# Last cross attention of a decoder: the fourth batch's values made between the heads' first maxima

## What is computed

```python
Q = (query @ Wq.T + bq).reshape(b, sq, H, D).transpose(0, 2, 1, 3)
K = (key @ Wk.T + bk).reshape(b, sk, H, D).transpose(0, 2, 1, 3)
V = (value @ Wv.T + bv).reshape(b, sk, H, D).transpose(0, 2, 1, 3)
Q = apply_rope(Q, cos_q, sin_q)
K = apply_rope(K, cos_k, sin_k)
scores = jnp.einsum('bhqd,bhkd->bhqk', Q, K) * SCALE
scores = jnp.where(mask[:, None, None, :] == 0, neg_inf, scores)
attn = jax.nn.softmax(scores, axis=-1)
out = jnp.einsum('bhqk,bhkd->bhqd', attn, V)
```

## Time and profile before

| | us |
|---|---|
| median of 3 runs | 1824.99 |
| lowest and highest | 1813.83 and 1825.43 |
| profiled execution | 1820.29 |
| its span | 1818.4 |
| PE, DVE, ACT, POOL busy, share of the span | 92%, 75%, 57%, 38% |
| projections of this phase | about 1023 to 1128 |
| heads of this phase | about 1127 to 1703 |

### The profile page before, as it was taken

How to read it: one execution, slowest core, us unless ns; L and a number is a source line. 1 busy time by engine, 2 the same in 40 slices (tenths; PEclk the granted TensorE clock), 3 DMA queues, 4 the chain that set the end, 5 groups by cost and what they waited for, 6 DMA issues and landing times. The chain is left out here.

```text
span 1818.4 us, 35284 instructions
## 1 busy us (share of the span) xinstructions
PE 1664.5 (92%) x13824; PEld 912.9 (50%) x13824; DVE 1363.4 (75%) x2337; ACT 1043.8 (57%) x1748; POOL 686.0 (38%) x771
## 2 busy tenths in 40 slices
PE   8998999989999998879999887799999999999996
PEld 4786677668888886423333654122222222223564
DVE  4535888756666665868885779999999999995664
ACT  4322655436566554337777333277888888887542
POOL 2783777024445443423340343215412121111453
PEclk9999999989999998969999999599999999999998
DMA  6163999777877763621110466221201011000001
GB/s 222 55 221 125 318 314 326 241 268 300 310 293 293 290 263 124 205 69 29 37 35 5 152 202 195 49 65 54 73 20 38 20 27 30 19 20 1 24 12 35
DMA packets 111693, 244.55 MB, mean 134 GB/s; under 512 B 27890, under 2 KB 80630, under 8 KB 107908
## 3 DMA queue, kind: packets, MB, share of 16 engines
q1 hardware_dynamic: 84712, 204.56, 32.1%
q0 software_dynamic: 24176, 35.12, 7.3%
q10 hardware_dynamic: 2640, 2.62, 0.4%
HBM read 180.27 MB, written 61.38 MB: 133 GB/s over the span
## 5 line engine op out<-in xcount | busy, mean ns | idle before, releaser
L2205 DVE TENSOR_REDUCE Eh_maxima<-Eh_max 128x2 f32<-128x802 f32 x512 | 474.8, 987 | 21.6 <-PE Eh_max L2077 16.7
L2193 ACT ACTIVATE Eh_probs<-Eh_pair 128x1024 f32<-128x1024 f32 (+1 forms) x288 | 287.5, 998 | 112.5 <-PE Eh_pair L2124 112.4
L2077 PE MATMUL Eh_max<-Eh_KS,Eh_QS 49*128 49x401 f16 x1024 | 197.7, 357 | 44.9 <-DVE Eh_maxima L2205 41.1
L2146 PE MATMUL Eh_av_ps<-Eh_probs,E_V 128*17 128x512 f32 (+1 forms) x1664 | 223.0, 609 | 0.0
L1537 PE MATMUL C_y<-C_x_high,C_W 128*128 128x256 f16 (+1 forms) x1536 | 214.8, 253 | 8.9 <-ACT C_gate L1597 7.4
L1537 PE MATMUL C_y<-C_x_low,C_W 128*128 128x256 f16 (+1 forms) x768 | 180.5, 252 | 0.0
L2193 ACT ACTIVATE Eh_probs<-Eh_single 128x512 f32<-128x512 f32 x272 | 161.7, 594 | 28.0 <-PE Eh_single L2124 27.8
L2205 DVE TENSOR_REDUCE Dh_maxima<-Dh_max 128x2 f32<-128x1024 f32 x128 | 152.0, 1221 | 31.9 <-PE Dh_max L2093 30.7
L1915 POOL DMA_DIRECT2D Eh_KS<-E_kd x64 | 37.1, 579 | 354.0 <-PE Eh_pair L2124 349.1
L2077 PEld LDWEIGHTS Eh_max<-Eh_KS,Eh_QS 49*128 49x128 f16 x1024 | 50.5, 94 | 233.1 <-DVE Eh_maxima L2205 198.2
L1537 PEld LDWEIGHTS C_y<-C_x_high,C_W 128*128 128x128 f16 x1536 | 139.0, 98 | 22.3 <-ACT C_gate L1597 9.6
(11 more groups left out here) (463 smaller groups left out, 3481.2 us busy)
## 6 DMA issues: line engine op xcount, KB each, us to landing
C_W<-w_split SPq DMA_DIRECT2D x24, 3072.0 KB
w_split<-B_w_parts SPq DMA_DIRECT2D x24, 768.0 KB, 8.1
Eh_KS<-E_kd POOLq DMA_DIRECT2D x64, 150.1 KB, 3.3
C_tail<-in_expert_tail_dram SPq DMA_DIRECT2D x24, 384.0 KB, 8.4
B_places<-in_w_experts_dram SPq DMA_DIRECT2D x10, 768.0 KB, 6.8
early_more<-in_w_experts_dram SPq DMA_DIRECT2D x8, 768.0 KB, 9.4
early_ctxT<-in_ctxT_dram SPq DMA_DIRECT2D x6, 800.5 KB, 6.0
early_ctxT<-in_w_experts_dram SPq DMA_DIRECT2D x6, 768.0 KB
```

Of the source, the lines that this page charges most:

```text
L2077: last = self.nc.tensor.matmul(bank[:, a, 0:self.cw], self.QS[r, slot, p, qt * P:(qt + 1) * P], self.KS[r, slot, p, k0:k0 + self.cw], star ...
L2146: last = self.nc.tensor.matmul(self.av_ps[u * STRIP:u * STRIP + VW, :], self.V[0:r, kt, unit * VW:(unit + 1) * VW], self.probs[0:r, self.b ...
L2193: self.nc.scalar.activation(dst, src, ACT.Exp, scale=1.0 / SCORE).then_inc(self.exp_done, 1)
L2205: self.nc.vector.tensor_reduce(self.maxima[:, g % 2, :, p * TPB + qt, c], self.max_ps[n % 2][:, :, 0:self.cw], AX_X, ALU.max).then_inc(sel ...
```

## The change

The value operations of the fourth batch are taken out of the projections: `value_ops` covers three batches. A new class `LateValues` makes them in the heads' part. `walk` yields "L" after maxima 4 to 16, one key tile each; PE makes the product in one of the two halves of `pair_ps`, the bank of the scores, and ACT copies it to `V`. The product of tile kt waits for the copy of tile kt - 2. PE waits for all 13 copies ahead of the first score. So that the context's halves and the weights outlive the projections, `halves`, `w_parts`, `parts`, `t` and `mask_row` are now views of the memory of `probs`, which is allocated ahead of both parts. PE's count `chunk_read` is left out for the last four chunks.

```diff
--- before.py
+++ after.py
@@ -1926,7 +1926,8 @@
 
 
 
-    def __init__(self, ctx, nc, name, n_keys, places, V, ATT, idents, tri, ahead, behind, order, start=None):
+    def __init__(self, ctx, nc, name, n_keys, places, V, ATT, idents, tri, ahead, behind, order, start=None, late=None, probs=None):
+        self.late = late
         self.nc, self.n_keys, self.causal, self.start = nc, n_keys, places.causal, start
         self.places, self.KS, self.QS, self.slots, self.R = places, places.KS, places.QS, places.slots, places.R
         self.V, self.ATT, self.tri, self.ahead, self.behind = V, ATT, tri, ahead, behind
@@ -1948,7 +1949,7 @@
         sb = lambda n, s, dt=F32: ctx.enter_context(nc.sbuf_tensor(f"{name}_{n}", s, dt))
         ps = lambda n, s, dt=F32: ctx.enter_context(nc.psum_tensor(f"{name}_{n}", s, dt))
         sem = lambda n: ctx.enter_context(nc.semaphore(f"{name}_{n}"))
-        self.probs = sb("probs", [P, self.turns * self.ring, S])
+        self.probs = sb("probs", [P, self.turns * self.ring, S]) if probs is None else probs
         self.maxima, self.top, self.neg_parts, self.neg_rows, self.inv = places.maxima, places.top, places.neg_parts, places.neg_rows, places.inv
         self.av = sb("av", [P, S])
         self.pair_ps, self.single_ps = ps("pair", [P, 2, S]), ps("single", [P, S])
@@ -1972,6 +1973,8 @@
         total_m, total_v = GROUPS * self.n_max, GROUPS * self.L
         for m in range(self.n_max + 2):
             yield "M", m
+            if self.late is not None and 0 <= m - LATE_AFTER < self.L:
+                yield "L", m - LATE_AFTER
         yield "R", 0
         for m in range(self.n_max + 2, self.n_max + self.ahead):
             yield "M", m
@@ -2153,6 +2156,10 @@
         n = 0
         for kind, k in self.walk():
             s, m = k if kind == "B" else (k, k)
+            if kind == "L":
+                self.late.product(pe, self.pair_ps[:, k % 2, :], k)
+            if kind in "SB" and s == 0 and self.late is not None:
+                pe.wait_ge(self.late.copied, self.L)
             if kind in "SB":
                 self.scores_of(pe, s)
             if kind in "MB":
@@ -2194,6 +2201,8 @@
 
     def scalar(self, act):
         for kind, k in self.walk():
+            if kind == "L":
+                self.late.copy(act, self.pair_ps[:, k % 2, :], k)
             if kind in "SB":
                 self.exponentials(act, k[0] if kind == "B" else k)
             if kind == "V" and k % self.L == self.L - 1:
@@ -2553,6 +2562,29 @@
     return [(ids[a], ids[b - 1] + 1) for a, b in zip(cuts, cuts[1:])]
 
 
+class LateValues:
+
+    def __init__(self, ctx, nc, V, weights, context):
+        self.nc, self.V, self.weights, self.context = nc, V, weights, context
+        self.ready, self.copied = (ctx.enter_context(nc.semaphore(f"E_late_{n}")) for n in ("ready", "copied"))
+
+    def product(self, pe, bank, kt):
+        r = key_rows(kt)
+        if kt >= 2:
+            pe.wait_ge(self.copied, kt - 1)
+        for k in range(KD):
+            for j, (x, y) in enumerate(((0, 0), (1, 0), (0, 1))):
+                last = self.nc.tensor.matmul(bank[0:r, 0:D], self.context(kt, x, k), self.weights[:, y, 1, k, :],
+                                             start=(k == 0 and j == 0), stop=(k == KD - 1 and j == 2))
+        last.then_inc(self.ready, 1)
+
+    def copy(self, act, bank, kt):
+        r, at = key_rows(kt), (B - 1) * H * VW
+        act.wait_ge(self.ready, kt + 1)
+        self.nc.scalar.activation(self.V[0:r, kt, at:at + H * VW].rearrange("p (h v) -> p h v", v=VW)[:, :, 0:DH],
+                                  bank[0:r, 0:D].rearrange("p (h d) -> p h d", d=DH), ACT.Copy, scale=1.0 / E_SCALE).then_inc(self.copied, 1)
+
+
 def spent_semaphores(nc):
 
     free = set(nc.free_semaphores)
@@ -2821,6 +2853,7 @@
 
 
 QUERY_PLACES = (6, 9, 12, 15)
+LATE_AFTER = 4
 
 
 def phase_cross1(nc, ctx, last, dram, X, XT, ident, ATT, weight_parts, loaded, weights_moved):
@@ -2847,23 +2880,36 @@
                         [(row_stored, 16)] + [(stored[i][m], 16 * (ITEMS // 2)) for i in range(2) for m in range(2)])
     tiles = [list(range(3 * c, 3 * c + 3)) for c in range(KC)]
     tiles[-1] = list(range(3 * (KC - 1), NK2))
-    value_ops = [(b, c, kts) for b in range(B) for c in range(KC)
+    value_ops = [(b, c, kts) for b in range(B - 1) for c in range(KC)
                  for kts in [tiles[c][0:2]] + [[kt] for kt in tiles[c][2:]]]
     ops_of = [[i for i, (b, c, _) in enumerate(value_ops) if b * KC + c == n] for n in range(KEYS)]
+
+    probs = ctx.enter_context(nc.sbuf_tensor("Eh_probs", [P, 18, S], F32))
+    room = probs[:].rearrange("p a s -> p (a s)").bitcast(F16)
+    halves = room[:, 0:2 * KD * S2]
+    w_parts = room[:, 2 * KD * S2:2 * KD * S2 + 4 * KD * D].rearrange("p (a b k d) -> p a b k d", a=2, b=2, k=KD)
+
+    def late_context(kt, a, k):
+
+        c = next(c for c in range(KC) if kt in tiles[c])
+        c0, w, at = starts[c], widths[c], kt * P - starts[c]
+        return halves[:, 2 * KD * c0:2 * KD * (c0 + w)].rearrange("p (a k w) -> p a k w", a=2, w=w)[:, a, k, at:at + key_rows(kt)]
 
     with ExitStack() as own:
         sb = lambda n, s, dt=F32: own.enter_context(nc.sbuf_tensor(f"E_{n}", s, dt))
         sem = lambda n: own.enter_context(nc.semaphore(f"E_{n}"))
         sems = lambda n, k: [sem(f"{n}{i}") for i in range(k)]
-        wq, w_parts = sb("wq", [P, KD, D]), sb("w_parts", [P, 2, 2, KD, D], F16)
+        wq = sb("wq", [P, KD, D])
         bq, bk = (sb(n, [P, 2]) for n in ("bq", "bk"))
         rotary = sb("rotary", [P, 4, S2])
         mask = sb("mask", [B, S2], I32)
-        mask_row, masked, any_kept = sb("mask_row", [B, S2], F16), sb("masked", [B, 2]), sb("any_kept", [P, B])
+        masked, any_kept = sb("masked", [B, 2]), sb("any_kept", [P, B])
         each, ones = sb("each", [B, B]), sb("ones", [B, P])
-        halves = sb("halves", [P, 2 * KD * S2], F16)
-        t, other = sb("t", [P, 2, 2, S]), sb("other", [P, 2, S])
-        parts = sb("parts", [P, 2, PARTS, 2, S], F16)
+        other = sb("other", [P, 2, S])
+        at = 2 * KD * S2 + 4 * KD * D
+        parts = room[:, at:at + 4 * PARTS * S].rearrange("p (i a m s) -> p i a m s", i=2, a=PARTS, m=2)
+        t = room[:, at + 4 * PARTS * S:at + 4 * PARTS * S + 8 * S].bitcast(F32).rearrange("p (i m s) -> p i m s", i=2, m=2)
+        mask_row = room[0:B, at + 4 * PARTS * S + 8 * S:at + 4 * PARTS * S + 8 * S + S2]
         staged = t[:].rearrange("p a m s -> p (a m) s")
         pair_ps = [own.enter_context(nc.psum_tensor(f"E_pair{i}", [P, 2, S], F32)) for i in range(2)]
         after = OutProjection(own, nc, "Do", X, XT, ATT, ident, dram["self_WoT"], None)
@@ -2969,8 +3015,9 @@
                                 last = mm(v_ps[i % 2][0:r, q, :], chunk(n, x, k, at, at + r), w_parts[:, y, 1, k, :],
                                           start=(k == 0 and j == 0), stop=(k == KD - 1 and j == 2))
                     last.then_inc(v_product, 1)
-                pe.wait_ge(v_product, ops_of[n][-1] + 1)
-                pe.sem_inc(chunk_read, 1)
+                if n < KEYS - RING:
+                    pe.wait_ge(v_product, ops_of[n][-1] + 1)
+                    pe.sem_inc(chunk_read, 1)
 
             after.tensor(pe)
             pe.wait_ge(w_high, 2)
@@ -3122,7 +3169,7 @@
         start = LastStart(last, nc, dram, X, XT, ATT, ident, beside)
         heads = Heads(own, nc, "Eh", S2, places, V, ATT, (ident, ident_half, None), None, 6, 2,
                       "M S M S M S S M V S M S M V M S S M V S M M S S M S V M S M S V M S S M V M S S M "
-                      "V M S S M V M S S M M S M S M S V M S M S V M S S M V S M S M S V R S M S M V S T", start)
+                      "V M S S M V M S S M M S M S M S V M S M S V M S S M V S M S M S V R S M S M V S T", start, LateValues(own, nc, V, w_parts, late_context), probs)
         start.use_banks(heads.max_ps)
         spent = spent_semaphores(nc)
         with nc.Block(no_gpsimd_drain=True) as block:
```

## The result

The changed kernel takes 1827.22 us in the median of 11 runs (1819.95 to 1833.97), the kernel before 1816.31 in the same comparison (11 runs, 1812.85 to 1825.43). The ratio is 1.0042, with a 95% interval of 1.0024 to 1.0059: a loss of 4 to 11 us, small but there. The medians themselves lie 10.9 us apart, at the upper end of that. The profiled execution took 1821.75 us, with a span of 1819.9.

A forecast was written before the change was run, and what follows sets the result against it. DVE was taken to bound the projections' end and the maxima. 0 (front) + 2.45 (ACT's wait) + 1.7 (half clock) = +4.15 us, put on 1822.6, gave 1827 us; range 1817 to 1836.

The forecast's parts named there:

- the sum: Whole kernel: 0 (projections' end) + 2.45 (ACT waiting for stores) + 1.7 (half-clock steps) = +4.15 us.
- the signs that I had named for a right prediction: First reduce unmoved, DVE idle 2 to 3 us before the eighth, later reduces 0.90 apart, row copies equally late.
- The front: End of the last batch's projections, up to the first reduce: DVE bounds it, so removing PE's value work costs 0.
- Price 0 to 0.3 us; I take 0: Last key product at a fallen clock: at most twice 2.44 us, ready about 1124.4, where DVE needs it at 1124.38.
- ACT's wait: Early maxima: ACT can't copy products before the projections' stores land at 1135.24, so DVE idles 2.45 us.
- The steps: One maximum plus one product: 1.59 us at half clock against DVE's 0.90, costing 1.7 us; at most 0.87 at full.
- the 1141 forecast: Among the maxima: dense products from about 1135.6 bring PE's clock back to full at about 1140.6.
- 0.30 a time, up to 2.7 us: Among the maxima: PE's possible cost of switching between full-array products and row-tiled maxima over 10 steps; taken as 0.
- 2.5 steps behind the wait: After the third product: 2.5 steps at the half clock, each 1.59 us instead of 0.90, 1.7 us in all.
- the first rival: Among the maxima: the clock stays low through all products, 2.45 + 6.9 = 9.35 us, 1832; chance 0.2.
- The second rival: First scores: the products keep the clock up into them, 4.15 - 4.57 = -0.4 us, 1822; chance 0.08.
- the 4.57: First step of the heads, 38.26 us against the second's 33.69: the difference taken as the half clock's cost there.

The follow-up runs named there:

- change_again: The changed kernel unaltered, measured a second time beside later runs; ratio to the kernel before 1.0026.
- early_load: The changed kernel with the last context chunk's load issued ahead of the last query item's store; ratio to the kernel before 1.0020.
- warm_front: The changed kernel with PE also making the fourth batch's value products in the projections, into a bank nobody reads; ratio to the kernel before 1.0017.
- left_out: The changed kernel without the fourth batch's value products anywhere, their columns of V constant ones; ratio to the kernel before 0.9990.
- act_free: The changed kernel with ACT waiting for the projections' stores ahead of its first exponential, not its first late copy; ratio to the kernel before 1.0032.
- double_late: The changed kernel with each late product made twice, 12 matmuls a tile instead of 6; ratio to the kernel before 1.0080.
- spread: The changed kernel with a late product after every second maximum (5 to 29) and ACT waiting for stores only before its first exponential; ratio to the kernel before 1.0001.
- late_end: The changed kernel with the late products after maxima 25 to 37, the last before the first score; ratio to the kernel before 1.0022.

## Why the prediction was right, and where it was off

The sign was right, and the size roughly: 4.15 us were forecast, and the two comparisons gave 7.6 and 4.7 (0.0042 and 0.0026 of 1820). The trace has 5.1 at the first exponential, change_again's 5.75. That the time came out at 1827.22 where 1827 was forecast is luck. I had put the sum on 1822.6 for the kernel before, whose median in that comparison was 1816.31; the 6.3 us too many there made up for the loss that was too small, 4.15 against 10.9 by the medians.

The mechanism was right in outline: the products among the maxima make DVE wait for PE, more so at the half clock, and ACT stands behind the stores. The terms were less right than their sum, and several of the signs that I had named for a right prediction didn't show. The front lost 1.25 us and not under 0.3, DVE idled 0.78 us ahead of the eighth reduce and not 2 to 3, the later reduces came 1.04 apart and not 0.90, and the copies of the rows weren't late by the same from step to step.

**The front.** "Price 0 to 0.3 us; I take 0" was too low: the traces of the change show 1.25 and 2.07 us. That DVE bounds the projections was right, as was that PE's clock might fall and the last product take up to twice its time. The error was its start. I let it start when DVE frees the bank, 11.4 us behind DVE's first operation on the last query item, though the row that I used had PE waiting for the context chunk. It started 13.7 behind, and took 3.76 and 4.68 us. It needed both, the late chunk and the low clock: early_load takes the first away and warm_front the second, and with either the loss is gone from the trace. How much of it reaches the end isn't settled. The traces have it at the last step, and no ratio shows it: left_out, with the front's loss alone, is at 0.9990.

**ACT's wait.** I had 2.45 us; act_free gets 0.3 to 0.5 us in the maxima, part of it from the clock, and the rows show 0.2 us in the change, 0.55 in change_again and 0.64 in warm_front. The wait was in place and PE did queue behind it. But I had counted the third product, at the half clock, as part of the wait, and the first two as free. PE was late on its own account by then: two slow steps ran from 1130.92 to 1134.6, while ACT waited anyway.

**The steps.** I had 1.59 us at the half clock; it is 1.84. I had at most 0.87 at the full one, which would have hidden them; it is 1.04. By the columns streamed alone it would be 0.80. Of the 0.23 us between, about half lies ahead of a product and half ahead of a maximum: at the full clock a product starts 0.28 us behind its maximum, where two 401-column matmuls side by side stream for 0.16, and the next maximum 0.76 behind the product, whose six matmuls stream for 0.64. That is the end "0.30 a time, up to 2.7 us" that I kept and didn't take; it cost 1.4 (ten steps of 0.14). In double_late, with twelve matmuls a product, the step of 1.69 us is over its columns by the same 0.24, so what is lost goes with the change from one kind to the other and not with the number of matmuls. double_late and spread show that PE is what bounds these steps. The clock was full at 1136, five microseconds before the 1141 forecast; PE had been dense since 1130.9 and not only since 1135.6. That alone doesn't set the moment. Behind the first late product the clock was full after 5 us in the change and 4 in change_again, but after 9 to 10 in warm_front and early_load, where PE was as dense but for one wait of 0.5 to 0.6 us. Two to five products were slow, by the trace, where the sum had 2.5 steps behind the wait, and each cost 0.94 us and not 0.69.

**The rivals.** The clock rose amid the products, so the first rival is out. By the rule of the Trainium skill beside it, in TensorE: Matmul & The Clock Gate, section "A second HAM failure mode: psum-queue depth-cycling", the clock would have swung; it stayed at 1.00 from 1136 to 1149. The second rival, the clock kept up into the scores, didn't occur. late_end brought it about and gained 0.34 us in the first step, not the 4.57 that I had read off two steps' lengths, because the clock fell among the scores. There, where PE has small waits for ACT, the page's rule does hold; the trace of late_end agrees with it. The 4.57 was off in itself: the second step, which I took for one at full clock, had 0.95, and against a step at 1.00 the first was 5.9 us longer (38.26 less 32.4).

What stays open: single traces differ by up to 3.5 us in the first step, and by 1.4 or 2.8 in any later one, with the moments at which the clock falls and comes back. No run sets these moments, so how much of the front's loss reaches the end is bounded only by left_out's interval, -0.0027 to +0.0008.

## What to carry to other kernels

Work moved into an engine's idle time must fit between two of the steps that wait on it, hand-over included: six matmuls between maxima that come every 0.90 us cost 3.9 us at one a step and 0.75 at one every second step. What the work had hidden must be looked at as well, since with it gone the engine idles, its clock falls, and a load that came just in time comes too late. Where the clock falls and rises at other moments from trace to trace, a comparison of two traces must go on well past the stretch that was changed: what looked like a gain of 3.5 us in one step was gone four steps later. And a wait that ends at a fixed moment costs only what isn't late already for other reasons.

## What the runs showed of the hardware

A change between full-array matmuls and row-tiled pairs cost PE about 0.12 us each way, at both clocks (1.84 against 1.61 us and 1.04 against 0.80 for a step, from the columns streamed). A step of the heads took 32.4 us at a granted clock of 1.00, 33.6 to 33.8 at 0.95 and 35.1 to 35.2 at 0.90. With PE kept busy in the projections the last key product ran at the full clock (2.46 us, warm_front), and with that work gone it took 3.41 to 4.68 us, at the half clock for part or all of it. How many products then ran at the half clock doesn't follow from that: it was five in warm_front, where the clock had been full up to 1134, and five in early_load, where it had been half from 1124 on.
